# Adding relu(h) into a copy of x ahead of the node pass of a two-layer graph network

## The reference

```python
# layer 0
h = x @ Wn.T + bn
e = edge_attr @ We.T + be
a = leaky_relu(sum((h[src] + e) * attn))
a = exp(a - segment_max(a, dst)[dst])
a = a / (segment_sum(a, dst)[dst] + 1e-16)
out = relu(segment_sum(h[src] * a, dst))
x = layernorm(x + out)
# layer 1, with dst' = src and neighbour = dst
mean = segment_sum(x[dst], src) / max(count(src), 1)
x = layernorm(x + x @ W1.T + b1 + mean @ W2.T + b2)
```

## Time and profile before

| | us |
|---|---|
| median of 3 runs | 1634.99 |
| lowest, highest | 1634.67, 1636.19 |
| profiled execution | 1637.05 |
| span of the profile | 1635.3 |

### The profile page before, as it was taken

The page is one execution under the profiler, slowest core; times in us unless marked ns, Lnnn a source line. Parts: engine busy times, 40 slices in busy tenths (PEclk is TensorE's granted clock), DMA queues, the critical chain, the costliest instruction groups (busy, mean ns, idle before and its releaser), DMA issues. The chain is left out here.

```text
span 1635.3 us, 29664 instructions
## 1 busy us (share of the span) xinstructions
PE 1409.0 (86%) x7910; PEld 1163.3 (71%) x7910; DVE 1081.9 (66%) x3942; ACT 835.0 (51%) x1870; POOL 887.8 (54%) x929
## 2 busy tenths in 40 slices
PE   5589688999999999999599998998855989899885
PEld 4478477887777778888477777777634777777774
DVE  8888888899999998888656656556532333233231
ACT  6556955566666677777433443343321434334333
POOL 1054742133333356443227777777766777777774
PEclk9899999999999999999799999999967999999998
DMA  3554134499999999999522333333323443433431
GB/s 81 148 104 113 59 82 101 169 349 358 362 357 353 350 347 326 337 326 320 171 65 92 104 101 102 105 109 104 102 87 96 121 114 110 119 116 111 120 97 59
DMA packets 119503, 280.00 MB, mean 171 GB/s; under 512 B 26464, under 2 KB 47335, under 8 KB 119431
## 3 DMA queue, kind: packets, MB, share of 16 engines
q1 hardware_dynamic: 77804, 193.81, 36.0%
q0 software_dynamic: 40128, 85.10, 16.8%
q10 hardware_dynamic: 1498, 0.27, 0.1%
HBM read 144.13 MB, written 142.28 MB: 175 GB/s over the span
## 5 line engine op out<-in xcount | busy, mean ns | idle before, releaser
L1243 PE MATMUL bank<-w1T,xT 128*128 128x256 f32 (+1 forms) x2368 | 594.3, 381 | 0.0
L1243 PEld LDWEIGHTS bank<-w1T,xT 128*128 128x128 f32 (+1 forms) x2368 | 413.1, 191 | 76.3 <-issue 0.8
L436 POOL DMA_INDIRECT order_scratch<-pay,rank_i x200 | 197.6, 988 | 248.5 <-DVE rank_i L832 87.7
L552 ACT ACTIVATE yout<-bank,nmr,rstd 128x256 f32<-128x256 f32 (+1 forms) x592 | 300.3, 578 | 1.8 <-DVE nmr L741 1.8
L898 DVE BATCH_NORM_STATS2 stats<-bank 128x6 f32<-128x512 f32 (+1 forms) x296 | 199.2, 687 | 132.1 <-PE bank L1243 132.0
L543 ACT COPY xT<-bank 128x512 f32<-128x512 f32 x396 | 232.1, 588 | 95.2 <-PE bank L1233 78.6
L430 POOL DMA_INDIRECT out_rows<-yout,idx_out x200 | 200.4, 1002 | 82.9 <-issue 58.2
L547 ACT ACTIVATE std<-stats,eps_c 128x4 f32<-128x4 f32 (+1 forms) x271 | 81.0, 299 | 277.7 <-DVE stats L898 274.9
L671 ACT COPY agg<-bank 128x257 f32<-128x257 f32 x200 | 74.2, 371 | 287.7 <-PE bank L1311 252.0
L427 POOL DMA_INDIRECT X<-in_x,idx_src x100 | 97.3, 973 | 218.5 <-DMA X<-in_x,idx_src 148.0
L1240 PE MATMUL bank<-bias,ones 128*128 128x256 bf16 x692 | 189.9, 274 | 11.9 <-ACT yout L552 9.7
(11 more groups left out here) (180 smaller groups left out, 1955.7 us busy)
## 6 DMA issues: line engine op xcount, KB each, us to landing
xin<-in_x SPq DMA_DIRECT2D x97, 512.0 KB, 5.5
x_scratch<-xin SPq DMA_DIRECT2D x97, 512.0 KB, 4.0
out_rows<-yout SPq DMA_DIRECT2D x97, 512.0 KB, 4.7
kB<-keys_scratch SPq DMA_DIRECT2D x50, 256.0 KB
kB<-sorted_scratch SPq DMA_DIRECT2D x50, 256.0 KB, 3.4
aggn<-low_digits_scratch SPq DMA_DIRECT2D x50, 128.0 KB
xin<-in_edge_attr SPq DMA_DIRECT2D x12, 512.0 KB, 5.4
order_scratch<-pay,rank_i POOLq DMA_INDIRECT x200
```

The lines of the kernel that those rows point to most:

```text
L436: g.indirect_dma_start(out=order_dram[k], out_offset=bass.IndirectOffsetOnAxis(ap=rank_i[k][:, t:t + 1], axis=0), in_=pay[:, t, :], in_off ...
L552: a.activation(yout[hu][0:rows, j, :], bank_of(j // 2)[0:rows, (j % 2) * D:(j % 2 + 1) * D], ACT.Identity, bias=nmr[0:rows, slot, j:j + 1] ...
L1243: ins = mm(to, buf[:, jj, c, 0:n], w[:, c, :], start=False, stop=i == len(terms) - 1 and c == 1)
```

## The change

- A table z takes the place of `x1_scratch`. SP copies x into it through the four `yout` buffers, one group of 512 rows per step: 4 steps at the start, 12 after the fourth load of edge features, 16 between the key spreads of the dst sort, 14 in one piece at the first round of the src sort and 16 between its other spreads, the rest after it.
- The x rows of the sources are gathered right after the order by dst is known (`ORDER_AT` = 12, in the src sort), four in flight; the scatters of the order are no longer held back. The softmax chain follows.
- The DST loop runs before the node pass. It ends at h: ScalarE writes relu(h), and GpSimd adds it into z by indirect DMAs with `compute_op=ALU.add`, each round's after the former round's have landed. Edges that are not the last of their key go to spare rows behind the table, at distinct places. Its node rows, their normalisation, product and scatter are gone.
- The node pass reads z instead of x and stores y alone. In it stand the scatter of the src order, its index columns (`HOOK` = 24) and, from group 32 on, the gathers of all 100 tiles of neighbour rows of z into X.
- The SRC loop gathers own rows of z, and normalises own rows itself. Neighbours are normalised inside the aggregation: `sel` holds 1/std, and two columns of X behind the row, std and mean, give the count and what is to be subtracted (XW = 258). Scales are done two tiles at a time.

```diff
+            def copy(n):
+                for c in range(copied[0], min(copied[0] + n, G + 2)):
+                    if c < G:
+                        wait(sp, s_cout[c % 4], 16 * (c // 4))
+                        sp.dma_start(full(yout[c % 4])[0:parts(c)], grp(x, c, parts(c))).then_inc(s_cin[c % 4], 16)
+                    if c >= 2:
+                        h = c - 2
+                        sp.wait_ge(s_cin[h % 4], 16 * (h // 4 + 1))
+                        sp.dma_start(grp(z_dram, h, parts(h)), full(yout[h % 4])[0:parts(h)]).then_inc(s_cout[h % 4], 16)
+                copied[0] = min(copied[0] + n, G + 2)
+            copy(4)
...
+                if c == 4:
+                    copy(COPY_FIRST)
                 wait(sp, s_eau, EC * (c - 3))
...
+                    if k == SRC and q == 0:
+                        copy(COPY_ONEHOTS)
+                    elif q % 3:
+                        copy(1)
...
+            for q in range(2):
+                load3(DST, q)
+            copy(G + 2)
+            for q in range(2, Q):
+                load3(DST, q)
+            for u in range(4):
+                sp.wait_ge(s_zsc[u], 16 * GT * len(range(u, Q, 4)))
...
+            for t in range(T):
+                pool.wait_ge(s_add[SRC], t + 1)
+                wait(pool, s_xg[t % FLIGHT], 16 * (t // FLIGHT))
+                gather(X[:, t, 0:D], x, column(idx_src[DST], t), s_xg[t % FLIGHT])
...
+            for q in range(Q):
+                pool.wait_ge(s_relu, 2 * q + 2)
+                if q:
+                    pool.wait_ge(s_zsc[(q - 1) % 4], 16 * GT * ((q - 1) // 4 + 1))
+                for j in range(GT):
+                    g.indirect_dma_start(out=z_dram, out_offset=column(idx_out[DST], GT * q + j), in_=xin[q % 4][:, j, :],
+                                         in_offset=None, compute_op=ALU.add).then_inc(s_zsc[q % 4], 16)
+                order_src(2)
...
+            pool.wait_ge(s_idx, 2)
+            pool.wait_ge(s_agg[DST], T)
+            for t in range(T):
+                pool.wait_ge(s_x1, GT * (HOOK + 8 + (G - HOOK - 14) * t // T))
+                wait(pool, s_nb[t % 2], 16 * (t // 2))
+                gather(X[:, t, 0:D], z_dram, column(idx_dst[SRC], t), s_nb[t % 2])
...
+                    wait(act, s_zsc[hu], 16 * GT * counted(m, u, -1, 4))
+                    for p in range(2):
+                        act.wait_ge(s_h, 2 * h + p + 1)
+                        a.activation(xin[hu][:, 2 * p:2 * p + 2, :].rearrange("p j d -> p (j d)"), rbank(par, p)[:, :],
+                                     ACT.Relu).then_inc(s_relu, 1)
...
+                if in_range(q, 0, Q):
+                    dve.wait_ge(s_xs[u], 16 * GT * (m + 1))
+                    moments(u % 2, lambda p: own[:, 2 * p:2 * p + 2, :], P, s_ost)
                 if in_range(q, 2, Q + 2):
-                    y_stats(SRC, q - 2, m, u, -2, lambda p: rbank(u % 2, p))
+                    dve.wait_ge(s_er, 2 * (q - 2) + 2)
+                    moments(2 + u % 2, lambda p: halves(rbank(u % 2, p)[:, :]), P, s_est)
+                if in_range(q, 0, Q - 2):
+                    neighbour_stats(q + 2, u)
+                if in_range(q, 0, Q):
+                    dve.wait_ge(s_osq, q + 1)
+                    invert(u % 2, P, n_m[u % 2] + counted(m, u, 0, 2) + 1)
+                    normalise(own, u % 2, P, s_ex1)
```

692 lines of the change are left out of this document (315 added, 377 removed).

## The result

The changed kernel takes **1665.1 us** (median of 4 runs, 1660.1 to 1668.3) where the kernel before takes 1634.8 us (4 runs, 1633.8 to 1636.2): the ratio is 1.018, 95% interval 1.015 to 1.021. It is slower by 30 us; the forecast was 1508 us, and the time lies far outside its range. The profiled execution took 1660.1 us with a span of 1658.3 us.

A forecast was written before the change was run, and what follows sets the result against it. Bounds taken: memory, then TensorE in the node pass; GpSimd in both edge loops. Sorts +18, copy and gathers +139, softmax -21, DST loop -208, drain +21, node pass -11, SRC loop -67: together -129, to 1508 us; range 1470 to 1590.

The forecast's parts named there:

- the tail: From the SRC loop's last product to the end of the span: stays at 18.5 us.
- Step (1): Edge features: twelve copy steps ahead of the fifth load delay their end by 14 us, to 78; bounds 0 and +20.
- Step (2): Both sorts: copy steps add 5 us each, the block of 14 adds 4, moved node-pass work saves 10; SRC sort ends at 329.
- rival A: Sorts: copies hold up key spreads on SP's queue, 2 us for each of 32 steps, 1558 us in all; chance 0.15.
- Step (3): Behind the sorts: gathers until 437 us, softmax over at 450, copy at 355 GB/s until 465, third DST round at 468.
- Step (4): DST loop: TensorE 8.3 us, additions landing after 3.5, 8.7 us a round; 206 us from the third round, ending at 674.
- Rival B: DST loop: the accumulating scatter lands late, at 6.5 us, a round is 11.6, +67, 1575 us; chance 0.14.
- Step (5): Drain from DST loop into node pass 21 us, starting it at 695; then 4.78 us a group, end at 1168.
- Step (6): SRC loop: TensorE bounds at 12.6 us a round, 25 rounds 316 us plus 3 for the start; last product at 1487.
- rival E: SRC loop: own rows gathered late because buffers free late, the round stays at 15.3 us, 1575 in all; chance 0.02.
- Rival D: SRC loop: VectorE's 11.4 us plus waits for ScalarE and TensorE make 14.5 us a round, +47, 1555 us; chance 0.09.
- Rival C: DST loop: accumulating scatters go one at a time, 19.1 us a round, +239, 1747 us, slower than before; chance 0.06.

The follow-up runs named there:

- direct copy run: The changed kernel with x copied into the table by one DRAM to DRAM transfer a step, instead of a load and a store: 1588.5 us, ratio 0.973.
- the plain scatter: The changed kernel with the DST loop's scatters writing relu(h) over the rows instead of adding it: 1609.2 us, ratio 0.985.

## Why the prediction was wrong

The structure was right and its order of events too. The sizes of its terms were not, and all but the node pass (5 us shorter) erred to the same side: features 6, sorts 73, copy and gathers 16, DST loop 7, drain 34, SRC loop 19, and 2 in the tail. The sum of the differences is 152 us. One reading was too wide: the chain in the earlier trace rows adds up to 24% of the span and begins at 1228 us, so it shows GpSimd ahead only in the SRC loop; that GpSimd sets the DST loop rests on its 292 issues of 1.28 us in 400 us.

**Step (1), features.** Forecast +14, came +20. The fifth load was to start near 58 and land at 64; it was issued at 61.9 and landed at 69.5, and the rest took 14.7 us, as forecast. Between 17 and 62 us the DMA moved 321 GB/s at a share of 0.98, not 355. Right in kind, 6 us off.

**Step (2), the sorts: the step that failed most.** "170 GB/s on top of 116, below 350, so I put only 5 us on each sort and 4 us on the block" asked whether the DMA would be full. It never was (0.68 to 0.74), and the sorts lost some 40 us each against the kernel before. What was asked too little is where the spread stands: behind 1 MB on the same queue, with 3.9 us for a group and 7.6 us for its landing. The text had the mechanism as rival A, at 2 us for each of 32 steps, 64 us, and a chance of 0.15; against the run without copy in the sorts it came to 85. Against the step's numbers (5 + 5 + 4 - 10) the miss is 34 us in the DST sort and 39 in the SRC sort. The 10 us taken off for the moved start of the node pass were too much: the SRC sort takes 103 us without copy steps and took 109 before, so at most 6.

**Step (3), copy and gathers.** Forecast: 124 us from the last lookup to the first aggregation; measured 140. The gathers took 180 us instead of 150 (1.8 us each, four in flight, each landing after 6.3 us and not 4.7). That the third round would wait for the copy's end didn't matter; there is no stall there. The reasoning behind 355 GB/s, that the memory is the limit, falls: between 341 and 372 us of the direct copy run the DMA moved 308 GB/s at a share of 0.99, and the 270 of them that are copy (0.524 MB every 1.94 us) were both read from memory and written to it, some 580 GB/s in all. The prediction said of the two ceilings named in the Trainium skill, DMA: Bandwidth & Descriptors (Where 436 GB/s comes from), that the trace agrees with the 358 of one core's share of HBM; the direct copy has far more memory traffic than that, and what held where the DMA was full was 308 to 362 GB/s through the DMA engines, under either figure.

**Step (4), DST loop.** Forecast 8.7 us a round and 206 us from the third round; the whole loop took 228 instead of 221. The 206 us are not the sum of their terms: 22 rounds of 8.7 and one of 6 are 197, and 206 takes 23 rounds and 6, so this step had 9 us to spare by accident, and against its own terms it missed by 16. TensorE's 8.3 us were right, as the 209 to 210 us of three experiments show. The issue of an accumulating scatter was put at 1.28 us, from plain ones, though the text says that no row shows one; the landing alone got bounds. It is 1.88 us from one issue to the next and 3.9 for the landing (forecast 3.5). With three issues ahead of the last, its landing and 0.7 us to react, a round is 3 x 1.87 + 3.9 + 0.7 = 10.2 us; by issues alone it is 4 x 1.88 + 2 x 1.28 = 10.1 us too. **Rival B** had the right place and the wrong cause: the landing was nearly right, the issue was not, and the two order scatters, named as what covers the landing, were themselves the second bound.

**Step (5), drain.** Forecast 21, came 55: the step that failed second. It took GpSimd to be at TensorE's heels when the loop ends. A round 1.9 us longer over a ring of four buffers leaves it four groups behind, and GpSimd issues its last addition 42 us after TensorE's last product. Against the plain scatter the slow rounds cost 19 us in the loop and 36 here: most of the loss shows where the loop is over. Without them, the drain is 19 to 22 us in four experiments: the forecast's own number. The node pass at 4.78 us a group came to 468.4 us, as forecast.

**Step (6), SRC loop.** Forecast 319 from the node pass's end, came 338. Of the 319, 24 rounds and the last products, 310 us, were to lie between the first W2 product and the last W1 product, and 9 ahead of them. When the gathers are ahead the rounds take 306 us; in the kernel after they take 319, of which the gathers cost some 9, which is **rival E** in small, at a place that it didn't name, GpSimd's own queue. The other part is the way into the loop, 18 us for 9: a first round with empty buffers and, for part of it, the lower clock. **Rival D** was wrong: VectorE has 235 us of work in 319. **Rival C** was wrong: additions overlap, issued 1.88 us apart with 3.9 us of landing.

**The range** was the second fault. It held A, B or D alone, and left their sums out as 0.15. But A and B are no rare accidents that exclude each other; both come from work on one engine's queue that was costed too low, the copy by its bandwidth and not by its place, the additions at the issue time of plain scatters. Their terms, at the size measured, are 73 and 41 us over the forecast, and together with the smaller ones they fill the 129 us of gain that were forecast and 23 us more.

## What to carry to other kernels

A queue that has bandwidth to spare can still cost its full latency: before putting large transfers on a queue that also carries small ones with a deadline, lay the landing time of the small ones against the time of one round, and put them ahead or elsewhere. Where an engine behind a ring of buffers is slower than the one that feeds it, look for the loss behind the end of the loop too, not only in it (36 us behind it here and 19 in it); and when taking one suspect away changes nothing, look whether another of the same length stands behind it before clearing the first. A table that is only copied should go from DRAM to DRAM, since the DMA engines then carry each byte once instead of twice (51.2 MB less here, and a step every 1.94 us instead of 4.1).

## What the runs showed of the hardware

- An accumulating indirect DMA holds GpSimd for 1.58 us (100 of them, 1.554 to 1.713), a plain one for 0.99, with the same 128 rows of 1 KB; they follow each other every 1.88 and 1.27 us, and land after 3.7 to 5.4 us, median 3.9, against 2.5 (kernel after and plain scatter).
- Large transfers, each counted once, came to 321 to 347 GB/s at a DMA share of 0.96 to 0.98 where one end is SBUF (347 over 288 us of the kernel before, with 362 in its best slice; 321 and 336 in the kernel after), and to 308 at 0.99 where both are DRAM (31 us of the direct copy, beside gathers); there the memory carried both directions at once.
- In the groups in which the kernel before took 1927 and 1938 us, engines paused between instructions that, by the rows, nothing held. One piece of VectorE's softmax chain, which runs at 0.3 us an instruction in the kernel after (542.28, 542.61, 542.87), reads there (order scatters out of the loop):

```profile
603.92 0.29 DVE L750 TENSOR_SCALAR tmp_r<-krow,ccol 100x128 f32<-100x128 f32 x1 [0.68 <-DVE ccol L1094]
605.33 0.23 DVE L750 TENSOR_SCALAR tmp_r<-tmp_r 100x128 f32<-100x128 f32 x1 [1.12 <-DVE tmp_r L750]
```

Each instruction there starts 1.4 us after the one before. The DMA share is 0.04 around it (575 to 600 us). In the run of the same group with the later SRC scatters the same piece falls into the copy, at a share of 0.98, and runs at the 0.3 us of the kernel after. A quiet DMA alone doesn't bring them: with the direct copy, where the kernel before takes 1635 us, the piece runs at 0.3 us at a share of 0.03. The cause isn't in the rows and stays open.
